# Adapter stage: x stacked by head for one-pass scores and projections, values folded with the output weights

## The reference, cut to what matters

```python
query = x @ Wq                                   # 8 heads of width 20
hs    = mha(query, enc @ Wk, enc @ Wv)           # 73 context keys
ca_q1 = (ca^T @ Wq_ca)[:, indices]               # 4 tokens -> 96 different rows, repeated to 512
ca_hs1 = mha(ca_q1, x, x)                        # keys and values are x itself, 512 of them
ca_hs2 = mha(ca_hs1 @ Wq, ca @ Wk_ca, ca @ Wv_ca)   # 4 keys
x = (hs + ca_hs2) @ Wout + b_out + x
```

## Time and profile before

| what | value |
|---|---|
| time, median of 3 runs | 1044.96 us (1041.37 to 1046.05) |
| the profiled execution | 1045.93 us, its span 1044.0 us |
| PE busy | 994.2 us, 95% of the span |
| DVE, ACT, POOL busy | 691.5, 596.7, 373.4 us |
| the adapter | from 0 to about 162 us of the span |
| its PE busy | 146.25 us of 162.00 |

### The profile page before, as it was taken

How to read it: one execution, slowest core, us unless ns; L and a number is a source line. 1 busy time by engine, 2 the same in 40 slices (tenths; PEclk the granted TensorE clock), 3 DMA queues, 4 the chain that set the end, 5 groups by cost and what they waited for, 6 DMA issues and landing times.

```text
span 1044.0 us, 17924 instructions
## 1 busy us (share of the span) xinstructions
PE 994.2 (95%) x6560; PEld 710.1 (68%) x6560; DVE 691.5 (66%) x1162; ACT 596.7 (57%) x1349; POOL 373.4 (36%) x488
## 2 busy tenths in 40 slices
PE   7999988999999999999999999999989999999998
PEld 4566655666667666667666667666646589999887
DVE  2766735777674677674677674677653879999563
ACT  2676734666773666773666773666753555455442
POOL 2566612444341344341344341343330024444220
PEclk9999977999999999999999999999999999999999
DMA  6300140000000000000000000000000340000000
GB/s 143 83 2 1 38 109 1 2 1 1 1 2 1 1 1 2 1 1 1 1 1 2 1 1 2 1 1 2 1 1 1 103 113 2 1 1 2 1 26 26
DMA packets 25370, 17.65 MB, mean 17 GB/s; under 512 B 8565, under 2 KB 24101, under 8 KB 25285
## 3 DMA queue, kind: packets, MB, share of 16 engines
q1 hardware_dynamic: 25285, 16.52, 6.2%
HBM read 11.26 MB, written 1.31 MB: 12 GB/s over the span
## 4 chain that ended last, share of the span: by engine, by line
PE 64%; DVE 10%; ACT 4%; issue 4%; POOL 1%; DMA 0%; SPq 0%; DVEq 0%; ACTq 0%; POOLq 0%
PE banks L409 13%; PE banks L396 12%; PE banks L382 11%; PE banks L416 4%; PE banks L224 3%; ACT sa_probs L499 3%; PE banks L227 2%; PE banks L225 2%; PE banks L226 2%; PE banks L1621 2%; PE banks L1913 2%; DVE sa_negmax L571 2%; DVE ca_top L1756 2%; DVE ca_probs L1761 1%; PE banks L232 1%
## 5 line engine op out<-in xcount | busy, mean ns | idle before, releaser
L639 POOL TENSOR_SCALAR sa_probs<-sa_probs,sa_inverse 128x512 f32<-128x512 f32 x320 | 216.9, 692 | 376.2 <-DVE sa_inverse L575 376.0
L499 ACT ACTIVATE sa_probs<-banks,sa_negmax 128x512 f32<-128x512 f32 x320 | 215.6, 685 | 164.8 <-DVE sa_negmax L571 164.7
L571 DVE TENSOR_REDUCE sa_negmax<-banks 128x2 f32<-128x1024 f32 x160 | 188.8, 1218 | 13.1 <-PE banks L382 10.4
L396 PEld LDWEIGHTS banks<-ident,sa_probs 128*128 128x128 f32 x1280 | 146.2, 142 | 55.2 <-issue 27.8
L396 PE MATMUL banks<-ident,sa_probs 128*128 128x128 f32 x1280 | 174.4, 277 | 9.7 <-ACT sa_turned L510 5.3
L580 DVE COPY sa_turned<-banks 128x512 f32<-128x512 f32 x160 | 110.1, 688 | 78.7 <-PE banks L396 78.6
L409 PE MATMUL banks<-sa_turned,sa_v 128*64 128x512 f32 x640 | 155.5, 607 | 0.0
L382 PE MATMUL banks<-sa_k_parts,sa_q_parts 64*128 64x512 f32 x960 | 136.8, 417 | 1.9 <-ACT sa_probs L499 1.9
L510 ACT COPY sa_turned<-banks 128x512 f32<-128x512 f32 x160 | 94.2, 589 | 31.6 <-PE banks L396 29.6
L382 PEld LDWEIGHTS banks<-sa_k_parts,sa_q_parts 64*128 64x128 f32 x960 | 86.5, 190 | 31.5 <-issue 14.6
L409 PEld LDWEIGHTS banks<-sa_turned,sa_v 128*64 128x64 f32 x640 | 38.8, 137 | 75.1 <-issue 73.9
(11 more groups left out here) (214 smaller groups left out, 1730.5 us busy)
## 6 DMA issues: line engine op xcount, KB each, us to landing
w_o<-in_L_xattn_wo SPq DMA_DIRECT2D x2, 800.0 KB, 8.9
out<-x SPq DMA_DIRECT2D x4, 320.0 KB, 2.4
w_q_t<-in_L_xattn_wq_t SPq DMA_DIRECT2D x1, 1120.0 KB, 9.9
fold_values<-ca_turned SPq DMA_DIRECT2D x5, 192.5 KB
x<-in_x SPq DMA_DIRECT2D x1, 960.0 KB, 5.6
fold_values<-ca_probs SPq DMA_DIRECT2D x4, 192.5 KB
w_q_t<-in_L_xattn_wq SPq DMA_DIRECT2D x1, 640.0 KB, 5.6
w_o<-in_L_xattn_wk SPq DMA_DIRECT2D x1, 640.0 KB, 8.0
```

Of the source, the lines that this page charges most:

```text
L396: last = pe.transpose(b_turn[e][:, q * P:(q + 1) * P], probs[:, j % 2, e, q, k * P:(k + 1) * P], ident[:])
L499: act.activation(probs[:, j % 2, e, q, :], b_scores[u % 2][:, e, :], ACT.Exp, bias=negmax[:, u % RING, e:e + 1], accum_out=total[:, u % RI ...
L571: dve.tensor_reduce(negmax[:, u % RING, :], b_scores[u % 2], AX_X, ALU.max, negate=True).then_inc(s_max.sem, 1)
L639: pool.tensor_scalar(probs[:, j % 2, e, q, :], probs[:, j % 2, e, q, :], inverse[:, u % RING, e:e + 1], 1.0, ALU.mult, ALU.mult).then_inc( ...
```

## The change

x is no longer padded for the turn. `x_stacked` holds each head in 64 columns: x rounded (to the format fp32r), the rest x minus rounded, rounded again, and four zeros. Turned, this makes four pieces of 128 rows (`NX` = 4) instead of two. The token queries and the query weights are stacked likewise (rounded, rounded, rest), so one fp32r matmul gives all three products. `scores1` uses 64 rows a head; `project_queries` is four fp32r matmuls instead of two float32 ones. ACT rounds x twice (`round_x`), DVE makes the rest (`rest_x`), for batch b + 2 at the end of slot k = 3. `x_pad` has one buffer and is filled at k = 1.

The second part: for each batch, the values spread by head are multiplied with the output weights (`fold_values`, 8 matmuls of 160 columns at k = 2), so `products` and `copy_heads` vanish, the 584 probabilities are turned in four full pieces and one of 72 rows, and `project_out` is a chain of five matmuls with 128 rows, into which the token part is merged. POOL spreads the values at k = 3 and the keys at k = 0 (one buffer each).

```diff
-        out += [("probs", u - 1, g) for g in range(G)] if 1 <= u <= units else []
+        out += [("probs", u - 1, 0)] if 1 <= u <= units else []
         if k == 0 and b + 1 < B:
-            out += [("x", b + 1, g) for g in range(G)]
+            out += [("x", b + 1, c) for c in range(NX)]
...
-            out += [("expanded", b - 1, 0)]
+            out += [("expanded", b - 1, 0)] + [("folded", b - 1, i) for i in range(2)]
...
+            for r in range(3):
+                sp.dma_start(wq_ca[:, :, r * HD0:(r + 1) * HD0], by_head(w("Wq_ca"))).then_inc(s_w, 16)
+            sp.dma_start(wq_raw[:], t["wq_stacked"]).then_inc(s_stacked, 16)
...
+                for c in range(NX):
+                    last = pe.matmul(ring.bank(banks, item), wq_s[:, c, g * P:(g + 1) * P], x_t[:, b % 2, c, :], start=(c == 0), stop=(c == NX - 1))
...
+                    rows = slice(e * HS, (e + 1) * HS)
+                    last = pe.matmul(banks[e][0:CTX, :], q1[rows, p, b, :], x_t[rows, b % 2, p, :], start=True, stop=True)
...
+            def fold_values(b):
+                at = lambda i: slice(i % 3 * D, (i % 3 + 1) * D)
+                of_group = lambda g, i, n: v_diag[:, (i + g) * P:(i + g) * P + n]
+                pe.wait_ge(s_wo, 16 * N_WO)
+                pe.wait_ge(s_vd.sem, s_vd.at(b, 0))
+                for half, parts in enumerate(((0, 1, 2), (3, 4))):
...
+                for i in range(CH - 1):
+                    pe.matmul(out_of(u), turned[:, u % TR, i * P:(i + 1) * P], folded[:, i, :], start=(i == 0), stop=False)
+                pe.matmul(out_of(u), turned_end[:, b % 2, q, :], folded[:, CH - 1, :], start=False, stop=True).then_inc(s_o.sem, 1)
...
+            turn_x(0, 0)
+            turn_x(0, 1)
+            pe.wait_ge(s_scaled.sem, s_scaled.at(0, 0))
+            for c in range(NX):
+                bank = (b_small, b_s1)[c // 2][:, c % 2, :]
+                last = pe.matmul(bank[:, 0:B * CTX], flat(wq_ca1[:, 2 * c:2 * c + 2, :]), flat(tokens[:]), start=True, stop=True)
...
                 if k == 0 and b + 1 < B:
-                    turn_x(b + 1, 0)
-                    turn_x(b + 1, 1)
+                    for c in range(NX):
+                        turn_x(b + 1, c)
...
+            def round_x(b):
+                heads = lambda r: x_s[:, :, :, r * HD0:(r + 1) * HD0].rearrange("p q h c -> p (q h) c")
+                if b > 0:
+                    ring.wait_made(act, ("x", b - 1, NX - 1))
+                act.copy(heads(0).bitcast(F32R), x[:, b * QT:(b + 1) * QT, :].rearrange("p q (h c) -> p (q h) c", h=H0)).then_inc(s_xhi.sem, 1)
+                act.wait_ge(s_xhi.sem, s_xhi.at(b, 0))
+                act.copy(heads(2), heads(0)).then_inc(s_xhi2.sem, 1)
...
                 if k == 3 and b + 1 < B:
                     copy_queries(b + 1, 1)
+                if k == 3 and b + 2 < B:
+                    round_x(b + 2)
...
+            def rest_x(b):
+                heads = lambda r: x_s[:, :, :, r * HD0:(r + 1) * HD0].rearrange("p q h c -> p (q h) c")
+                dve.wait_ge(s_xhi.sem, s_xhi.at(b, 0))
+                dve.tensor_tensor(heads(1).bitcast(F32R), x[:, b * QT:(b + 1) * QT, :].rearrange("p q (h c) -> p (q h) c", h=H0),
+                                  heads(0), ALU.subtract).then_inc(s_xlo.sem, 1)
...
-                if s == NU - 1:
+                if s == NU:
+                    dve.wait_ge(s_vd.sem, s_vd.at(B - 1, 0))
                     next_ln.standardize(dve, 0)
```

More of the change, by code:

```diff
@@ L896, in scores1 @@
                 if p == 0:
[L897 to L898 removed]
+                    for c in range(NX):
+                        ring.wait_copied(pe, ("x", b, c))
                 if s == 0:
[L900 to L901 removed]
+                    pe.wait_ge(s_q1.sem, s_q1.at(0, 1))
                 else:
@@ L1004, in project_out @@
                     ring.wait_copied(pe, ("expanded", b, 0))
-                for g in range(G):
-                    pe.matmul(out_of(u), heads[:, u % HR, g, :], wo[:, g, :], start=(g == 0), stop=False)
-                pe.matmul(out_of(u), probs2x[rows, q * P:(q + 1) * P], v2_out[rows, :], start=False, stop=True).then_inc(s_o.sem, 1)
+                    ring.wait_copied(pe, ("folded", b, 1))
+                for i in range(CH - 1):
+                    pe.matmul(out_of(u), turned[:, u % TR, i * P:(i + 1) * P], folded[:, i, :], start=(i == 0), stop=False)
+                pe.matmul(out_of(u), turned_end[:, b % 2, q, :], folded[:, CH - 1, :], start=False, stop=True).then_inc(s_o.sem, 1)
             pe.wait_ge(s_ident, 16)
@@ L1029, in _ @@
             for g in range(G):
+                last = pe.matmul(b_small[:, g, 0:NK], flat(wv[:, g * HG:(g + 1) * HG, :]), ctx_t[:, :, 0:SE], start=True, stop=True)
+            last.then_inc(s_vp.sem, 1)
+            for g in range(G):
                 project_queries(0, g)
-            for b in range(B):
-                bank = (b_out, b_token)[b // 2]
-                last = pe.matmul(bank[0:SE, b % 2 * HC:(b % 2 + 1) * HC], ctx_t[:, b, 0:SE], flat(wv[:]), start=True, stop=True)
-                if b % 2 == 1:
-                    last.then_inc(s_vp.sem, 1)
             for s in range(SLOTS):
@@ L1053, in _ @@
                 if 0 <= u - 1 < NU:
-                    turn_probs(u - 1, 0)
-                    turn_probs(u - 1, 1)
-                if 0 <= u - 2 < NU:
-                    products(u - 2)
+                    turn_probs(u - 1)
                 if k == 0 and b + 1 < B:
-                    turn_x(b + 1, 0)
-                    turn_x(b + 1, 1)
+                    for c in range(NX):
+                        turn_x(b + 1, c)
                 if k == 0 and 1 <= b <= B:
@@ L1320, in _ @@
                     copy_x(b + 1)
+                if k == 2 and 1 <= b <= B:
+                    copy_folded(b - 1)
                 if k == 3 and b + 2 < B:
-                    pad_x(b + 2)
+                    rest_x(b + 2)
+                if k == 1 and 1 <= b < B:
+                    pad_x(b)
                 if s == NU - 2:
```

335 lines of the change are left out of this document (196 added, 139 removed).

## The result

The changed kernel is slower by 1.1%: 1055.92 us in the median of four runs (1054.10 to 1056.66), beside 1044.89 of four runs of the kernel before on the same chip. The ratio is 1.0107, with a 95% interval of 1.0093 to 1.0122. The forecast was 1055 us. The profiled run is the fastest of the four, 1054.10 us with a span of 1052.3, so it stands 8.3 us of span above the profiled run of before.

The account below looks back on a forecast made before the run. PE's own work bounds the middle slots, with a nearly as slow wheel behind it, and waits decide the last stretch. 5 - 0.5 + 2.5 + 1.9 + 2.3 - 1 = +10.2 us gives 1055 us; 8-in-10 range 1040 to 1072.

Parts of the forecast that it names:

- the wheel: Loop of inverses1, POOL's scaling, turn_probs1, project_out, scores, shift: 6.4 us a slot from slot 7, 4.8 before.
- the ring: Four x turns share two places; the third waits for ACT's copy of the first, a 1.5 us bubble; the fourth for DVE.
- the x turns: Slots 4 and 8 take 9.4 and 9.5 us; with clock dips +2.5 (slots 4 to 7) and +1.9 (8 to 11).
- the start: Up to slot 1: three new issues +2 us, doubled token queries +2.6; in all +5, between +2 and +8.
- slots 12 to 14: The wheel, and PE's own work at k = 2: 6.4 + 7.3 + 8.0 = 21.7 us for 19.44, +2.3.
- slots 1 to 3: 4.8 + 4.8 + 4.85 us by the wheel and 2.3 for a cold beginning: 16.8 for 17.28, -0.5.
- the tail: Slot 15 to the adapter's outputs: changes put even, 1 us won by a denser PE; -1, between -5 and +5.
- dip of the clock: After the waits at slots 4 and 8 PE's clock falls once each, costing 1.7 us; lower bound 0.
- a cold beginning: Extra 2.3 us put on slots 1 to 3.
- A: Rival: ring waits and the wheel hidden by slack behind PE; -11 in loop, +3 at start; 1037 us, chance 0.17.
- C: Rival: PE idle 1.5 to 2 us in every slot, clock low over slots 1 to 16; 1082 us, chance 0.09.
- B: Rival: start costs 5, the wheel turns in 6.1, bubbles near 0.5, no dip; 1045 us, chance 0.18.

Follow-up runs that it names:

- e4_start: Changed kernel with token-query weights on their own semaphore, x's second half loaded before the query weights, batch 1's x rounded before the query copies: 1053.86 us.
- e11_port: Changed kernel with POOL starting to spread the keys only after VectorE finishes the rest of the stacked query weights: 1056.00 us, ratio 1.0114.
- e12_all: Changed kernel with the edits of e4_start, e11_port, e1_out_late and e3_values_late together: 1042.34 us, ratio 0.9982 of the kernel before.
- e3_values_late: Changed kernel with POOL's spreading of a batch's values moved from k = 3 to k = 1 of the batch after: 1057.78 us, ratio 1.0147.
- e1_out_late: Changed kernel with project_out moved behind scores on PE and update behind shift and inverses1 on VectorE: 1052.84 us, ratio 1.0083.
- e5_before_late: Kernel before with project_out moved behind scores on PE and update behind shift and inverses1 on VectorE: 1049.33 us, ratio 1.0069.

## Why the prediction was right

The mechanism is the one forecast in kind: PE lost work and found no time in it, because the wheel over POOL, the ring at the x turns and a longer start stood next in line. That the time came out within 1 us is luck: the start and slots 12 to 14 cost 4.7 and 2.5 us more than forecast, slots 1 to 3, the tail and the rest of the span 2.8, 3.8 and 2.0 less, and these errors cancelled. Of the signs that I had named, `max1` did come behind `rest_x`; PE waited for POOL in slots 12 to 14 (0.69, 1.53 and 1.37 us), but not in 15. The start was at 36 us for 31, the third x turn waited 1.12 us for 1.5 or more, and the only dip of the clock between 40 and 100 us lay in slots 2 and 3.

**The start** was +9.7 for +5, beyond my upper bound of +8. The issues and the token queries were as I had them (11.07 for 8.58, and 5.48 for 2.92: 5 us in all). What I had counted as covered was not: 1.55 us for the stacked weights and 2.23 us for batch 1's x, which I had named but not priced. The doubled pieces of x cost 1.8 us behind the token queries and 2.7 us ahead of slot 1, at PE's lower level, and I had no price for them either. Against this stood 3.5 us: the wait of 1.38 us ahead of the first scores is gone (with it that stretch is 1.6 us shorter), these scores took 1.3 us less, and the projections 0.6, not the 3 us that I had set for them. `e4_start` took 5.3 us back by order alone, `e11_port` 0.8.

**Slots 1 to 3** were -3.3 for -0.5. I had added 2.3 us for a cold beginning, and 4.8 for slot 1, which took 3.45. Slots 2 and 3 took 5.2 and 5.3 us for 4.8; the clock fell there behind a wait of 1.07 us for POOL (0.88 over the stretch).

**The x turns.** The round costs 0.72 us (0.7 priced), the rest 0.83 (0.75). The bubble of slot 4 is 1.83 + 1.12, not 1.5, and falls on the second and third turn; I had left out that the second needs the ring place of the probabilities. Slot 8 has 0.87 and 1.12. On the other side **no dip of the clock** followed: both stretches are at 1.00. The 1.7 us that I had put there for each wasn't spent, though `e12_all` shows low clock behind the very same waits; one profile can't price such a term. That the sums of slots 4 to 11 match the forecast is an accident: the slots with the x turns took 10.48 and 10.61 us for 9.4 and 9.5, those with the folding 1.9 more than forecast each, and the other four 3.0 less together; this and the missing dips cancelled.

**The wheel.** Slots 12 and 13 took 6.42 and 7.23 us, for 6.4 and 7.3 forecast, but not by the wheel alone. In slot 12 PE waits 0.54 us more for a ring place, behind ScalarE's copy of the queries; in slot 13 it waits 1.53 us for POOL behind `spread_values` and `add_bias`, which I had not put on the wheel. `e3_values_late` moves the first of them, and slot 13 falls to 6.47 us. That the wheel is there too is shown by `e1_out_late`: with the outputs taken out of it slot 12 falls to 5.60 us, and slot 14's wait for POOL is gone. The k = 2 slot was the miss: 8.92, 9.89 and 10.54 us (slots 6, 10, 14) for 7.0, 8.0 and 8.0. I had taken the longer of the wheel and of PE's own work. In this slot they add: PE waits 1.37 us for POOL, then still has all of its work, and in the middle of the folding waits 0.89 us more, because its second half needs the ring place of the expanded probabilities, which ScalarE copies behind an exponential and two roundings of weights (0.44 and 0.45). That is the +2.5 us by which slots 12 to 14 missed. The chain of five took 1.38 us (129.44 to 130.82), my lower bound.

**The tail** was -4.8 for -1: chains of 1.36 us instead of products and chains at the low clock. The clock over this stretch is 0.90 for 0.74. Moreover the self-attention began at full clock, where before it began at the low one (first matmul 0.47 us for 0.76). The 2.0 us behind the adapter don't come from that: `e5_before_late` begins it at the low clock too (0.77) and takes 878.3 us from there, the changed kernel 878.0, the kernel before 880.4.

**The rivals.** A (work saved becomes time) is refuted by the idle time in the windows. C (low clock throughout) didn't come: the clock is 1.00 in slots 4 to 14. It is seen in part in `e4_start`, 0.82 over slots 12 to 14. The Trainium skill, TensorE: Matmul & The Clock Gate, section "A second HAM failure mode: psum-queue depth-cycling", has short idles swing the clock; here the clock falls behind waits of 0.9 to 1.8 us in some runs and not in others. B (no change) failed at the start and at the bubbles.

**VectorE's rest beside POOL.** The row that hinted at it showed no such case: VectorE's instruction beside POOL's 1.29 us was the copy of x, with one SBUF input. The rest of x took 0.82 and 0.83 us alone and 1.12 and 1.11 us beside POOL, and POOL's instruction beside it 1.45 and 1.44 for 0.86: VectorE's 0.3 us stand ahead of `max1` each time, far from the whole POOL instruction of that sentence. It bit harder at the start. The Trainium skill, SBUF — State Buffer, section "Who interferes with whom", says that a VectorE instruction with two SBUF inputs and one of GpSimd that reads SBUF contend for a port that one of them holds at a time. The trace agrees that they contend (2.27 us together, 1.27 and 1.17 apart), but not that the earlier runs on undisturbed: POOL's had begun 0.87 us ahead and itself took 2.06.

What stays open: why the clock falls behind a wait in one run and stays up behind the same wait in another, and in which stretches the four longer runs of `e5_before_late` lose their time. One profile of each can't tell it.

## What to carry to other kernels

When one engine is busy to the last tenth, work taken off it is worth only the distance to the next loop of waits; go around that loop and add up its pieces before cutting, and in a slot where the engine also has much work of its own, add the wait to the work instead of taking the longer of the two. A wait on such a loop can have two causes, and one edit alone may show nothing: here one gave 2 to 3 us and the other lost 4, and together they gave 6. Look at the clock of the stretch before calling such an edit a loss: where it was taken into account, the gains in the slots nearly added up. Where a change doubles the pieces that pass through a ring of buffers, count for every new piece whose copy it must wait for, and where on the copying engine that copy stands.

## What the runs showed of the hardware

- VectorE and POOL slow each other: VectorE's instruction with two SBUF operands (1024 elements) took 2.27 us beside POOL's and 1.27 alone; POOL's 2.06 and 1.80 beside it, 1.17 and 0.83 alone.
- The same waits leave the clock as it was or not. With 1.83 and 1.12 us of idle time in slot 4, eight transposes behind them took 1.09 us in the changed kernel and 1.97 in `e12_all`; the changed kernel's low stretch lay in slots 2 and 3 instead (0.88). The runs of one kernel lie up to 10 us apart, and in most kernels the longer ones have the lower mean clock: `e12_all` took 1038.91 us at 0.993 and 1047.49 at 0.985, `e5_before_late` 1042.84 at 0.985 and 1052.47 at 0.976. A mean that is lower by 0.008 over 1045 us is 8.4 us of PE's time at full clock, about the difference. An effect of 2 us can't be told from one profile.
- The self-attention and all behind it, the same code in every kernel here, took between 876.9 and 881.3 us from the first matmul on, with PE busy for 844.3 to 848.0 us of it; a comparison of spans has to leave that out.
- The four fp32r matmuls of 512 columns that make one query projection took 1.17 to 1.19 us at full clock, where the two float32 ones (four records) took 1.96.
